# Last pair reordered, blocks of M in rows of 256 columns, narrow filler products, W_lang in halves

## What is computed

```python
def reference(x, adj, W_lang, W_grav, W_V, W_O, gate_logit, log_sigma):   # x: 32 x 256 x 512
    z_l, z_g, v = x @ W_lang.T, x @ W_grav.T, x @ W_V.T
    zn = z_l / norm(z_l)
    A_l = maximum(zn @ zn.T, 0) * not_eye
    d2 = maximum(sq + sq.T - 2 * z_g @ z_g.T, 0)          # sq: squared norms of z_g
    A_g = exp(-d2 / (2 * sigma ** 2)) * not_eye
    K = w * row_stochastic(A_l * adj) + (1 - w) * row_stochastic(A_g * adj)
    return layernorm(x + (K @ v) @ W_O.T)
```

## Time and profile before

| | us |
|---|---|
| device time, three runs | 653.62, 654.11, 655.98 (median 654.11) |
| device time of the profiled execution | 655.62 |
| its span | 653.9 |
| TensorE busy | 641.2 |
| VectorE busy | 533.6 |
| ScalarE busy | 383.4 |
| GpSimd busy | 136.1 |

### The profile page before, as it was taken

The page is one execution under the profiler, slowest core; times in us unless marked ns, Lnnn a source line. Parts: engine busy times, 40 slices in busy tenths (PEclk is TensorE's granted clock), DMA queues, the critical chain, the costliest instruction groups (busy, mean ns, idle before and its releaser), DMA issues.

```text
span 653.9 us, 10726 instructions
## 1 busy us (share of the span) xinstructions
PE 641.2 (98%) x2858; PEld 530.1 (81%) x2858; DVE 533.6 (82%) x1430; ACT 383.4 (59%) x707; POOL 136.1 (21%) x288
## 2 busy tenths in 40 slices
PE   8999999999999999999999999999999999999995
PEld 7888888888888888888888888888888888887774
DVE  5774979798897978888797978979797988978785
ACT  5453545656665565657556565756656566555665
POOL 2711011211211121121212112121211112112022
PEclk9999999999999999999999999999999999999999
DMA  9311757484665749386575928566683847454542
GB/s 294 76 54 51 176 160 175 119 246 104 210 158 174 197 134 246 85 256 140 165 177 174 226 80 259 127 193 150 186 209 111 250 104 229 109 167 140 161 136 106
DMA packets 141509, 106.48 MB, mean 163 GB/s; under 512 B 40112, under 2 KB 115632, under 8 KB 141488
## 3 DMA queue, kind: packets, MB, share of 16 engines
q1 hardware_dynamic: 140768, 104.40, 57.5%
q0 software_dynamic: 288, 1.05, 0.5%
q10 hardware_dynamic: 432, 0.79, 0.3%
HBM read 65.80 MB, written 40.40 MB: 162 GB/s over the span
## 4 chain that ended last, share of the span: by engine, by line
PE 92%; DVE 3%; DMA 2%; SPq 1%; ACT 1%; issue 1%; DVEq 0%; ACTq 0%
PE bank L1397 58%; PE bank L1485 17%; PE bank L1490 14%; PE bank L1442 2%; DMA work<-k_spill 1%; DVE p_lo L1033 1%; SPq L439 1%; DMA x_spill<-xs 1%; DMA r_row<-r_spill 1%; DMA xs<-in_L_gnn_W_lang 1%; PE bank L1420 0%; DVE work L1091 0%; DVE work L1148 0%; PE bank L1423 0%; SPq L422 0%
## 5 line engine op out<-in xcount | busy, mean ns | idle before, releaser
L735 ACT ACTIVATE p_hi<-bank,m_scale 128x512 fp32r<-128x512 f32 x128 | 85.8, 683 | 54.5 <-PE bank L1490 53.5
L1033 DVE SCALAR_TENSOR_TENSOR p_lo<-bank,m_scale,p_hi 128x512 fp32r<-128x512 f32 x128 | 94.0, 747 | 18.6 <-ACT p_hi L735 18.6
L1490 PE MATMUL bank<-hT_lo,m_hi 128*128 128x512 f32 x384 | 107.8, 389 | 0.0
L1397 PE MATMUL bank<-wvo_hi,hT_hi 128*128 128x512 f32 x256 | 99.7, 389 | 0.0
L1397 PE MATMUL bank<-wvo_hi,hT_lo 128*128 128x512 f32 x256 | 99.6, 389 | 0.0
L1397 PE MATMUL bank<-wvo_lo,hT_hi 128*128 128x512 f32 x256 | 99.6, 389 | 0.0
L1397 PE MATMUL bank<-p_hi,hT_hi 128*128 128x512 f32 x256 | 99.6, 389 | 0.0
L1397 PE MATMUL bank<-p_lo,hT_hi 128*128 128x512 f32 x256 | 99.6, 389 | 0.0
L608 POOL TENSOR_TENSOR rnorm<-norm,minus_half 128x2 f32<-128x2 f32 x32 | 34.8, 1088 | 245.1 <-DVE norm L1061 245.1
L1490 PEld LDWEIGHTS bank<-hT_lo,m_hi 128*128 128x128 f32 x384 | 72.1, 188 | 15.0
L739 ACT CAST v_hi<-bank 128x512 fp32r<-128x512 f32 x60 | 32.4, 590 | 62.6 <-PE bank L1397 62.6
(11 more groups left out here) (163 smaller groups left out, 1253.6 us busy)
## 6 DMA issues: line engine op xcount, KB each, us to landing
x_blk<-in_x SPq DMA_DIRECT2D x128, 128.0 KB, 3.5
x_spill<-xs SPq DMA_DIRECT2D x30, 512.0 KB, 3.8
xq<-x_spill SPq DMA_DIRECT2D x120, 128.0 KB, 3.5
x_nat<-in_x SPq DMA_DIRECT2D x30, 512.0 KB, 4.5
out_y<-y SPq DMA_DIRECT2D x30, 512.0 KB, 4.1
k_spill<-work SPq DMA_DIRECT2D x30, 256.0 KB, 2.2
work<-k_spill SPq DMA_DIRECT2D x120, 64.0 KB, 2.3
r_row<-r_spill SPq DMA_DIRECT2D x32, 128.0 KB, 3.5
```

Of the source, the lines that this page charges most:

```text
L735: nc.scalar.activation(p_hi[:, :, j, g, :], src[:].rearrange("p (b n) -> p b n", b=2), ACT.Copy, scale=m_scale[:, g, j:j + 1]).then_inc(pr ...
L1033: nc.vector.scalar_tensor_tensor(out=p_lo[:, :, j, g, :], in0=src[:].rearrange("p (b n) -> p b n", b=2), scalar=m_scale[:, g, j:j + 1], in ...
L1397: last = pe.matmul(dst, lhsT, rhs, start=(n == 0), stop=(n == len(steps) - 1))
L1490: last = pe.matmul(pbank(k)[:], md_hi[:, g, 0] if i == 0 else m_hi[:, g, i, c], lo[i], start=False, stop=(i == DT - 1))
```

## The change

Five things. WARM goes from 6 products of 512 columns to 35 of 128, on a fill of 128 x 128. The first two parts of W_lang come as halves of 64 partitions, the lower from SP and the upper from ScalarE; parts 2 and 3 both from SP. Block rows 1 to 3 of M are all 256 wide: besides row 0, the blocks (1, 1), (1, 3), (2, 1), (2, 2), (3, 2) and (3, 3) are computed, and each MIRROR unit turns two blocks, once the last UPPER unit's copy is made. The last pair has new orders on SP, GpSimd, ScalarE, VectorE and TensorE. Nothing of the loop over pairs changes but the choice between m_lo and m_hi as stationary operand.

```diff
+        def made(i, j):
+            return (i, j) in ((0, 1), (0, 2), (0, 3), (1, 3), (2, 1), (3, 2))
+        def row_blocks(row, i):
+            if i == 0:
+                return row
+            if i == 1:
+                return row.rearrange("p (k two n) -> p k two n", two=2, n=P)[:, :, 1]
+            return row[:, (i - 1) * P:(i + 1) * P]
...
-        WARM = 6
+        WARM = 35
...
+        def load_eighth(queue, k, side):
+            rows = slice(side * P // 2, (side + 1) * P // 2)
+            queue.dma_start(raw[L][rows, k], w_lang[k * P:(k + 1) * P, :][rows]).then_inc(w_loaded[L][k], 16)
...
-            for k in (0, 2):
+            for k in range(2):
+                load_eighth(sp, k, 0)
+            for k in range(2, DT):
                 load_quarter(sp, k)
...
+            spread_r(q, 1)
             return_x(q, 1)
-            spread_r(q, 1)
             spill_k(q, 0)
+            return_k(q, 0)
+            load_x(q, 0)
+            spill_k(q, 1)
+            store(q - 1, 0)
+            return_k(q, 1)
+            store_r(p, 0)
             load_last(0)
             load_x(q, 1)
-            spill_k(q, 1)
-            return_k(q, 0)
-            load_x(q, 0)
-            store(q - 1, 1)
-            return_k(q, 1)
-            store(q - 1, 0)
-            store_r(p, 0)
             spread_r(p, 0)
             store_r(p, 1)
+            store(q - 1, 1)
+            spread_r(p, 1)
             load_last(1)
-            spread_r(p, 1)
             store(q, 0)
-            store_last(0, 1)
             store(q, 1)
             store_last(0, 0)
+            store_last(0, 1)
             store_last(1, 1)
...
-            nc.gpsimd.memset(kt_hi[:, 0].bitcast(F32), 0.0).then_inc(warm_ready, 1)
+            nc.gpsimd.memset(kt_hi[:, 0, 0, 0].bitcast(F32), 0.0).then_inc(warm_ready, 1)
...
-            for k in (1, 3):
-                load_quarter(act, k)
+            for k in range(2):
+                load_eighth(act, k, 1)
...
+            proj_hi_part(p, 0)
+            proj_hi_part(p, 1)
             squares(q - 1, 0)
...
+            normalise(q - 1, 0)
             proj_hi_part(p, 6)
             proj_hi_part(p, 7)
+            squares(q - 1, 1)
             gauss_scaled(q, 1)
-            normalise(q - 1, 0)
-            normalise(q - 1, 1)
+            save_x(p, 0, 0)
             proj_hi_part(p, 8)
-            save_x(p, 0, 0)
             save_x(p, 0, 1)
+            centre(p, 0)
             kt_hi_part(q, 0)
             save_x(p, 1, 0)
             save_x(p, 1, 1)
+            last_gauss(0)
+            centre(p, 1)
+            normalise(q - 1, 1)
             kt_hi_part(q, 1)
-            centre(p, 0)
-            centre(p, 1)
...
             last_squares(0, 1)
+            last_normalise(0, 0)
             last_squares(1, 0)
             last_squares(1, 1)
-            last_normalise(0, 0)
...
-            inverse_masked(q, 1)
+            gauss_masked(q, 0)
             gram(q, 0, L)
+            proj_lo_part(p, 0)
             turn_x(q, 1)
             cosine_masked(q, 0)
-            proj_lo_part(p, 0)
             gram(q, 1, G)
             proj_lo_part(p, 1)
-            gauss_masked(q, 0)
+            proj_lo_part(p, 2)
+            row_factors(q, 0)
+            gram(q, 1, L)
+            proj_lo_part(p, 3)
+            inverse_masked(q, 1)
...
             last_residual(0, 0)
             last_means(0, 0)
+            last_kt_lo_part(1)
             last_residual(0, 1)
...
-                    pe.wait_ge(prep_lo, prepared(UPPER, g, i - 1))
-                    for r in range(i):
+                    pe.wait_ge(prep_hi, prepared(UPPER, g, DT - 1))
+                    for r in [r for r in range(DT) if made(r, i)]:
...
-                pe.matmul(kv_bank[1][:], kt_hi[:, 0, 0, 0], in_kt(kt_hi, 0), start=True, stop=True)
+                pe.matmul(kv_bank[1][:, 0:P], kt_hi[:, 0, 0, 0], kt_hi[:, 0, 0, 0], start=True, stop=True)
...
-                    stationary = m_lo[:, g, i, c] if i < j else md_hi[:, g, i] if i == j else m_hi[:, g, i, c]
+                    stationary = m_lo[:, g, i, c] if made(i, j) else md_hi[:, g, i] if i == j else m_hi[:, g, i, c]
...
+            last_gram_turn(p, 0, G)
             last_gram_turn(p, 0, L)
             k_times_v(q, 0, 0)
             k_times_v(q, 0, 1)
-            last_gram_turn(p, 0, G)
             last_gram_turn(p, 1, G)
             last_gram_turn(p, 1, L)
             value(p, 1, 0, 1)
+            k_times_v(q, 1, 0)
+            k_times_v(q, 1, 1)
             pe.wait_ge(last_gram[0][L], 1)
             value(p, 1, 1, 0)
-            k_times_v(q, 1, 0)
             last_k_turn(p, 0)
-            k_times_v(q, 1, 1)
             pe.wait_ge(last_gram[0][G], 1)
             value(p, 1, 1, 1)
+            last_k_times_v(p, 0, 0)
             last_k_turn(p, 1)
-            last_k_times_v(p, 0, 0)
             last_k_times_v(p, 0, 1)
```

More of the change, by code:

```diff
@@ L139, in diagonal_blocks, with mirrored_blocks @@
             return (flat[:, 0:(DT - 1) * step].rearrange("p (i w) -> p i w", w=step)[:, :, 0:P], flat[:, (DT - 1) * step:])
+        def made(i, j):
[6 more added lines that the diff above has]
+            return row[:, (i - 1) * P:(i + 1) * P]
+        def mirrored_blocks(tile, i):
+            row = tile.rearrange("p (k n) -> p k n", n=P)
+            if i == 1:
+                return row.rearrange("p (a two) n -> p a two n", two=2)[:, :, 0]
+            return row[:, 0:2] if i == 3 else None
         def split_blocks(tile, g):
@@ L666, in _ @@
                 layer_norm(q, b)
-            for b, t in ((0, 1), (0, 0), (1, 0), (1, 1)):
+            for b, t in ((0, 0), (0, 1), (1, 0), (1, 1)):
                 last_spread(b, t)
@@ L698, in prep_hi_part @@
                 if kind == MIRROR:
-                    nc.scalar.copy(m_hi[:, g, i, 0:i * P], src[:, 0:i * P]).then_inc(mirrored, 1)
+                    if i == 2:
+                        for j in (0, DT - 1):
+                            c = slice(j * P, (j + 1) * P)
+                            last = nc.scalar.copy(m_hi[:, g, i, c], src[:, c])
+                    else:
+                        last = nc.scalar.copy(mirrored_blocks(m_hi[:, g, i], i), mirrored_blocks(src[:], i))
+                    last.then_inc(mirrored, 1)
                     return
                 if kind == UPPER:
-                    nc.scalar.copy(m_hi[:, g, i, i * P:], src[:, i * P:]).then_inc(prep_hi, 1)
+                    nc.scalar.copy(row_blocks(m_hi[:, g, i], i), row_blocks(src[:], i)).then_inc(prep_hi, 1)
                 else:
@@ L1341, in _ @@
             proj_lo_part(p, 7)
+            cosine_masked(q, 1)
+            row_factors(q, 1)
             kernel_sum(q, 1)
-            proj_lo_part(p, 8)
             diagonal(p, 0)
             turn_k(q, 0)
+            proj_lo_part(p, 8)
             turn_r(p, 0)
             kt_lo_part(q, 0)
-            turn_k(q, 1)
+            last_gram_sum(0, G)
             diagonal(p, 1)
             last_gram_sum(0, L)
+            residual(q, 0, 0)
+            turn_k(q, 1)
+            turn_r(p, 1)
+            residual(q, 0, 1)
+            last_gauss_masked(0)
             kt_lo_part(q, 1)
[L1352 to L1355, removed]
             last_gram_sum(1, G)
-            last_gauss_masked(0)
             last_inverse_masked(0)
@@ L1398, in products, with three_products @@
                 return last
-            def three_products(rows, stationary, moving, cols=slice(None)):
+            def three_products(rows, stationary, moving):
                 (sh, sl), (mh, ml) = stationary, moving
-                return [s for r in range(DT) for s in ((sh[:, r, rows], mh[:, r, cols]), (sh[:, r, rows], ml[:, r, cols]),
-                                                       (sl[:, r, rows], mh[:, r, cols]))]
+                return [s for r in range(DT) for s in ((sh[:, r, rows], mh[:, r]), (sh[:, r, rows], ml[:, r]),
+                                                       (sl[:, r, rows], mh[:, r]))]
             def emptied(u):
@@ L1435, in prepare @@
                 elif kind == UPPER:
-                    cols = slice(i * P, D)
-                    steps = three_products(rows, w_parts[g], w_parts[g], cols)
+                    hi, lo = w_parts[g]
+                    steps = [s for k in range(DT)
+                             for s in ((hi[:, k, rows], row_blocks(hi[:, k], i)), (hi[:, k, rows], row_blocks(lo[:, k], i)),
+                                       (lo[:, k, rows], row_blocks(hi[:, k], i)))]
                     for n, (lhsT, rhs) in enumerate(steps):
@@ L1441, in prepare @@
                             pe.wait_ge(w_lo_ready, DT * g + n // 3 + 1)
-                        last = pe.matmul(dst[:, cols], lhsT, rhs, start=(n == 0), stop=(n == len(steps) - 1))
+                        last = pe.matmul(row_blocks(dst[:], i), lhsT, rhs, start=(n == 0), stop=(n == len(steps) - 1))
                 elif kind == MIRROR:
```

(4 more changed lines are left out.)

54 lines of the change are left out of this document (22 added, 32 removed).

## The result

The changed kernel takes 652.84 us (median of 20 runs, 652.21 to 653.71) against 654.52 for the kernel before in the same comparison (20 runs, 653.61 to 656.46): ratio 0.9972, 95% interval 0.9963 to 0.998. That is 1.7 us faster where 4.7 were forecast, above the upper end of the range, and within the 0.5% that counts as no change.

What follows compares the result with a forecast made beforehand. TensorE, busy 641.2 of 653.9 us, was taken as the bound, idle only at both ends. Last pair -4.0, blocks -0.75, start 0 made -4.75: 650.9 from the profiled 655.62, 649.4 as median; range 646.7 to 652.3.

Steps and rivals of the forecast that it cites:

- The start: the failed step: TensorE's start: clock rises at 6.1, within the filler; first block ends at 10.1 against 10.05; taken as 0, -1.9 to +5.6.
- The third rival: Start: narrow filler does not count for the clock; +5.6 (655.0 us), or loss 3.8 (653.2); chance 0.08 for both.
- The rival of 0.108 us: Start: fillers 0.108 us apart also at the low level, 35 end at 4.9; 1.9 sooner, 647.5 us; chance 0.27.
- The halves of W_lang: Loads at the start: part 0 perhaps 0.5 us sooner, but filler covers it; taken as 0.
- The blocks of M: Three rows of 256 columns save 1.06 us over two matrices, less +0.3 for a new wait: -0.75.
- Strips with a gap: Block row 1 of M reads two strips: at worst +2.3 us, at best nothing; taken as 0.
- The new wait for ScalarE's copy: Turning of G's blocks waits for ScalarE's copy of the last row: +0.3 us, between 0 and +0.6.
- The last pair: New engine orders remove TensorE's three stops and shorten the ending: -4.0 us in sum.
- (a) to (c): Last pair: two early p_lo stops go, -2.1; third stop, for `centre`, goes, -1.3; new late TensorE wait, +0.2.
- (c): Last pair: VectorE's kt_lo of the second last K stands behind `last_residual(0, 0)`, giving TensorE +0.2 us of wait.
- (d): Last pair: late `store(q - 1, 1)` makes VectorE wait 0.4 us, covered by slack; taken as 0, +1.5 kept for range.
- (e): End: `store(q, 1)` goes out about 4 us before the last row is ready; between 0 and -1.4, taken as -0.7.

Runs made afterwards that it cites:

- tail_narrow35: The kernel before with the last pair's new orders and the 35 narrow filler products, old loads and old blocks of M: 653.31 us, ratio 0.9985.
- old_loads_narrow35: The changed kernel with W_lang loaded in whole quarters again, its 35 fillers of 128 columns kept: 652.88 us, ratio 0.9974 to the kernel before.
- f_wide6: The changed kernel with the old filler, 6 products of 512 columns and the wide fill: 651.44 us, ratio 0.9942 to the kernel before.
- tail_newloads: The kernel before with the last pair's new orders and the new loads of W_lang in halves, nothing else: 651.28 us, ratio 0.995.
- tail_wide8: The kernel before with the last pair's new orders and 8 fillers of 512 columns instead of 6: 649.32 us (0.9926); a second time 649.05 (0.9924).
- tail_blocks: The changed kernel with filler (6 of 512 columns) and W_lang loads put back, leaving new last pair and blocks of M: 649.21 us, 0.992 to the kernel before.
- b_tail: The kernel before with the new orders of the last pair on all five engines and no other part of the change: 649.61 us, ratio 0.9916.
- best_wide8: The changed kernel with 8 fillers of 512 columns and W_lang in whole quarters: 649.89 us, ratio 0.9923 to the kernel before.

## Why the prediction was wrong

**The start: the failed step.** The term was "I take 0", on the rise of the clock at 6.1, 5.0 us after unbroken work of any width. It measured +2.58 in the profiled executions, and about +4.1 by the medians (an estimate, above). The first half of the step was right: narrow products at the low level are 0.215 us apart, where 0.22 was taken. (The 0.46 us for the six wide fillers is an average with a first gap of 0.59; the others are 0.427 apart.) What failed is the assumption that this filler brings the clock's rise as wide products did. It does not: 35 or 120 of them end as they began, and the rise comes 2.65 us (the change; 3.0 in tail_narrow35, 3.5 in old_loads_narrow35, 3.8 after 120) behind the first 512-column product. The step's forecast of 25 fillers at 0.22 and the rest at half that was the test, and it failed in the form that the prediction itself named: spacing of one value throughout, and products slow past 9 us.

The third rival was this mechanism. Its higher price, +5.6, was too high; its lower one, +3.8, is near the 4.1 of the medians, and the 653.2 it gave is near the measured 652.84. That is in part luck, as two errors cancel: it put the rise 5.0 us behind wide work, where the change's profiled execution has 2.65, and it took the block before at 10.05, where the medians say 8.95. The clock row could not decide, since it stays full; only the first rows of TensorE could. The prediction gives no reason for its chance of 0.08. The one rise in view had come after products of 512 columns alone, so no row spoke for narrow ones, and a much higher chance was due.

**The rival of 0.108 us** is excluded. The Trainium skill (TensorE: Matmul & The Clock Gate, LDWEIGHTS) puts the load of 128 weight columns at 107 ns without naming a level; by it the filler would have ended at 4.9. The runs show such products 0.108 apart at the high level and 0.214 at the low one; the measurement decides, and the prediction's doubling was right.

**The halves of W_lang** were given "perhaps 0.5 us sooner" for part 0 and no cost because filler covers them. The cover was real (0.9972 against 0.9974). The rest was wrong: part 0's cast begins at 4.16 in the change and at 4.04 with whole quarters under the same filler, part 1's at 6.02 against about 4.6. Uncovered, that is 1.4 to 2.2 us (f_wide6, tail_newloads). Each request of half a quarter took 0.6 us to issue on SP (two in 1.22) and 0.75 on ScalarE (two in 1.49), a whole one 0.43 (two in 0.87), and part 1, which was its queue's first request, is now the second on both. Whether the issue alone explains the late landing was not tried.

**The blocks of M**: -0.75 forecast, -0.71 measured in the change. Strips with a gap cost nothing: 0.12 us a product, like the others. The new wait for ScalarE's copy was 0.56 where +0.3 net was taken, and the old one for hT_lo (0.36) went in exchange. What the forecast did not see is the wait for hT_lo that appears, in four of eight executions with the blocks (1.40, 1.32, 0.99 and 0.27 us), once TensorE is early enough or VectorE late enough. In the runs' times the gain of the blocks is too small to be told.

**The last pair**: -4.0 forecast, -5.09 measured. Between the first projection and the last product, what products start later than the usual distance of their kind adds up to 4.24 us before and 0.73 now: -3.5, where (a) to (c) had -3.2. The three stops were as forecast, and the new wait of 0.26 stands for the 0.2 of (c); what the sum lacked is a fourth stop of 0.31 us, inside the turning of the Gaussian gram behind the product at 627.54. (d), the late `store(q - 1, 1)`, cost TensorE nothing. (e) was mis-sized: from the last product to the end of the span 1.33 us went, where 0.8 was taken with the normalise of the first tile. `store(q, 1)` is out by 640.28, the last store is issued at 647.43, not 649.61, and SP's three start at 643.93. Of the remaining 0.25 us, 0.14 lie outside the stretch from the first projection to the end of the span; the rest is too small to place.

**The total**: +2.58, -0.71, -5.09 in place of 0, -0.75, -4.0; by the medians the first is about +4.1. On medians the change gained less than in the profiled executions, 1.7 against 3.2 us: the profiled execution of before, 655.62, was 1.1 us above its median of 20 runs, that of the change 0.4 below. Executions with the same start as before had the rise at 7.52, 10.05 and 10.98. That this wandering is what spreads the runs of the kernel before over 2.9 us, and those of the change over 1.5, is argued from the steady columns of the table, not shown.

**A kernel that beats both** is any with the new last pair, wide filler and W_lang in whole quarters: tail_wide8 at 0.9926 and 0.9924, tail_blocks at 0.992, b_tail at 0.9916, best_wide8 at 0.9923. Their intervals overlap, so the runs do not say which of them is best; all lie below the change's interval.

## What to carry to other kernels

Filler that is to bring TensorE's clock up should be of a form that rows show to do it, and the first rows tell: how long after the first real product do the products get faster? After eight fillers of 512 columns it was 0.6 to 1.4 us, within 35 of 256 it was before real work, after those of 128 it was 2.65 us or more. And one profiled execution is not enough to date a rise: hold it against the median of the runs. Price parts of a change against each other, not only against the kernel before: here one part hid another's cost (filler over late loads) while eating a third's gain. And when a stage gets faster, look at the next engine's list just behind it; hT_lo took from the blocks' gain in four executions out of eight.

## What the runs showed of the hardware

- Fp32r products of 128 columns are 0.108 us apart at the high level and 0.214 at the low one. Unbroken for 25.7 us, they left TensorE at the low level. Products of 256 columns did not: they are as close together at first, and changed about 5.3 us after the first.
- Counted from the start of the last unbroken stretch of products of 256 or 512 columns, the rise came after 2.65 us at the least (the change) and 6.2 at the most (b_tail, 4.82 to 10.98). With eight fillers of 512 columns and no stop it was at 5.53, 5.63 and 6.42; with six and a stop of half a microsecond at the first real product, at 7.52 (tail_blocks), 10.05 (before) and 10.98 (b_tail). These are three executions each, and the medians of b_tail and tail_wide8 do not differ (0.9916, 0.9926), so an effect of the stop is not shown.
- The row of granted clock was full at the start of every profile (in four of the fourteen only its last slice falls to 8), also where products of 512 columns took 0.63 us at 0.43 from start to start. At the start the clock is to be read from the products.
- VectorE's diagonal product (custom operation, 128 x 128) took 0.28 us alone and 0.8 to 1.4 when it began inside one of GpSimd's subtractions of v_lo, eleven times in eight traces. Each of the eleven ended 0.15 us after the subtraction that was running when it began, so it seems to wait for the whole of it; two that began in the last 0.1 us of one took 0.29. VectorE's own subtractions of 512 columns, which read one operand from a bank, kept their 0.69 beside the same work. This was seen, not tested by a run of its own.
